# A recurrent mixing layer with a routed expert layer behind it: the output bias added to x in memory by accumulating DMAs, and the row statistics of every block taken by accumulators and ScalarE's squares

## The reference

```
xk, xv, xr = x_prev + (x - x_prev) * tm{k,v,r}        # x_prev: x one token earlier
k, v, r = xk @ Wk + bk, xv @ Wv + bv, xr @ Wr + br
wkv = scan over the tokens of (k, v, time_decay, time_first)
x1 = layernorm(x + (sigmoid(r) * wkv) @ Wo + bo)      # bo: one row of 512 numbers
expert = argmax(softmax(x1 @ wg)); gate = its probability
out = layernorm(x1 + gate * (x1 @ W[expert] + b[expert]))
```

## Time and profile before

| | |
|---|---|
| median of 3 runs | 649.12 us |
| the profiled execution | 652.63 us, its span 650.8 us |
| mean granted TensorE clock of the span | 0.96 |
| TensorE matmul / weight load busy | 582.5 us (90%) / 430.4 us (66%) |
| VectorE busy | 552.7 us (85%) |
| ScalarE busy | 409.4 us (63%) |
| GpSimd busy | 280.3 us (43%) |
| DMA mean rate | 104 GB/s, 67.64 MB |

### The profile page before, as it was taken

The page is one execution under the profiler, slowest core; times in us unless marked ns, Lnnn a source line. Parts: engine busy times, 40 slices in busy tenths (PEclk is TensorE's granted clock), DMA queues, the critical chain, the costliest instruction groups (busy, mean ns, idle before and its releaser), DMA issues. The chain is left out here.

```text
span 650.8 us, 8971 instructions
## 1 busy us (share of the span) xinstructions
PE 582.5 (90%) x2484; PEld 430.4 (66%) x2485; DVE 552.7 (85%) x871; ACT 409.4 (63%) x759; POOL 280.3 (43%) x213
## 2 busy tenths in 40 slices
PE   0667788999999999999999999999998999898991
PEld 0455576667668767677866876875566778676771
DVE  7958898999999899899999989878969698556771
ACT  4246565566756747746775674846957676666883
POOL 5643552552454444445155244421041465555541
PEclk9779898999999999999999999989979999899996
DMA  8030010013104103202210410616834686676660
GB/s 307 18 129 2 1 65 0 1 36 126 34 2 158 37 1 113 64 16 89 72 32 13 150 33 0 227 36 255 259 100 143 185 240 206 204 208 198 201 195 4
DMA packets 36566, 67.64 MB, mean 104 GB/s; under 512 B 8560, under 2 KB 8560, under 8 KB 36532
## 3 DMA queue, kind: packets, MB, share of 16 engines
q1 hardware_dynamic: 30292, 48.29, 23.5%
q0 software_dynamic: 6240, 18.94, 9.1%
HBM read 50.17 MB, written 18.88 MB: 106 GB/s over the span
## 5 line engine op out<-in xcount | busy, mean ns | idle before, releaser
L1110 POOL TENSOR_TENSOR mixed<-unsplit,mixed 128x1024 fp32r<-128x1024 f32 x44 | 104.4, 2392 | 132.4 <-ACT mixed L764 132.4
L512 PE MATMUL kb<-mixed,w_kvr 128*128 128x512 f32 x384 | 99.0, 409 | 23.6 <-DVE mixed L1453 16.6
L512 PE MATMUL vb<-mixed,w_kvr 128*128 128x512 f32 x384 | 102.6, 418 | 14.6 <-DVE evn L1291 9.0
L694 PE MATMUL y_ps<-w_e_hi,xgT 128*128 x312 | 110.4, 414 | 4.2 <-DVE yo L1743 3.2
L512 PE MATMUL rb<-mixed,w_kvr 128*128 128x512 f32 x384 | 102.0, 416 | 5.6 <-DVE ee L1305 4.5
L512 PEld LDWEIGHTS kb<-mixed,w_kvr 128*128 128x128 f32 x384 | 74.4, 197 | 42.2 <-issue 16.2
L530 PE MATMUL y_ps<-w_o,rw 128*128 128x512 f32 x224 | 100.6, 592 | 0.0
L512 PEld LDWEIGHTS vb<-mixed,w_kvr 128*128 128x128 f32 x384 | 74.5, 198 | 36.1 <-DVE evn L1291 11.8
L512 PEld LDWEIGHTS rb<-mixed,w_kvr 128*128 128x128 f32 x384 | 73.5, 194 | 27.9 <-issue 5.7
L1120 POOL TENSOR_TENSOR ee<-ee,state 128x512 f32<-128x512 f32 x32 | 34.9, 1091 | 107.3 <-DVE state L1275 106.6
L1242 DVE SCALAR_TENSOR_TENSOR unsplit<-diff,vec,xb 128x512 f32<-128x512 f32 x96 | 72.1, 812 | 8.1 <-PE kb L512 6.1
(11 more groups left out here) (240 smaller groups left out, 1053.9 us busy)
## 6 DMA issues: line engine op xcount, KB each, us to landing
bias<-b_experts SPq DMA_DIRECT2D x39, 256.0 KB
w_e_raw<-w_experts SPq DMA_DIRECT2D x8, 1024.0 KB, 7.9
rows<-x SPq DMA_DIRECT2D x28, 256.0 KB, 2.6
x_rows<-rows SPq DMA_DIRECT2D x28, 256.0 KB, 2.1
xb<-xT SPq DMA_DIRECT2D x4, 1026.0 KB, 5.4
xb<-xT SPq DMA_DIRECT2D x3, 1024.0 KB, 5.0
w_raw<-w_square SPq DMA_DIRECT2D x2, 1024.0 KB, 10.2
xb<-xT SPq DMA_DIRECT2D x2, 512.0 KB, 5.0
```

The source lines that it names most:

```text
L512: mm = pe.matmul(bank, w_kvr[m][:, a, h, o:o + P], mixed[m][:, bb, h, :], start=(k == 0), stop=(k == 3 * CH - 1))
L694: mm = pe.matmul(y_ps[:, n % 2, :], xgT[n % 3][:, a, c, :], w[:, bass.ds(p, 1), c, :].rearrange("p u o -> p (u o)"), start=(c == 0 and (a, ...
L1110: pool.tensor_tensor(mixed[m][:, LO, 2 * hp:2 * hp + 2, :], unsplit[m][:, LO, 2 * hp:2 * hp + 2, :], mixed[m][:, HI, 2 * hp:2 * hp + 2, :] ...
```

## The change

The bias moves out of the matmuls. A new tensor in device memory, `x_biased`, gets a copy of x, 1 MB for each block, by a DMA of SP (memory to memory); then GpSimd issues an accumulating DMA that adds bo, broadcast over 512 rows, to that copy. `load_rows` and the last block's loads read `x_biased` in place of x. The bias matmuls, `bo2`, and bo's split at the start go away. The way to statistics that the block before the last has is used in all blocks: `add_rows` takes the accumulator, `average` replaces `statistics` and `aggregate`, and ScalarE's `deviation` squares the two row tiles into the tile `x1T`, which serves as scratch, before its Ln and Exp.

```diff
@@ sync @@
+            def copy_block(n, half):
+                sp.dma_start(sum_block[n], x_block[n]).then_inc(x_copied[half], 16)
-                    sp.dma_start(rows[:, j], x_v[n * TPB + j]).then_inc(row_loaded[j], 16)
+                    sp.dma_start(rows[:, j], sum_v[n * TPB + j]).then_inc(row_loaded[j], 16)
             (step)
                 load_x(i + 1, s.batch + s.half, 1 - s.half)
+                if not s.prev2:
+                    copy_block(i + 1, 1 - s.half)
                 if not s.prev:
+                    sp.wait_ge(x_summed[0], 16)
                     load_rows(0, range(TPB), first=True)
                 if s.prev2:
+                    wait_apart(sp, x_summed[1 - s.half], (s.batch + s.half) * 16)
+                    copy_block(i + 1, 1 - s.half)
                     load_rows(m, (0, 1))
             (start)
-            sp.dma_start(b_raw[:], bo).then_inc(bo_loaded, 16)
-            sp.wait_ge(b_lo, 1)
-            sp.wait_ge(bias_zero, 1)
-            for s in range(2):
-                sp.dma_start(bo2[s:s + 1, :].bitcast(F32), b_split[:, s, :].bitcast(F32)).then_inc(bias_moved, 16)
+            copy_block(0, 0)
             (last block)
+            sp.wait_ge(x_summed[0], BATCH * 16)
+            sp.wait_ge(x_summed[1], BATCH * 16)
-                sp.dma_start(rows_last[:, j], x_v[last * TPB + j]).then_inc(last_loaded, 16)
+                sp.dma_start(rows_last[:, j], sum_v[last * TPB + j]).then_inc(last_loaded, 16)
@@ tensor @@
-            def bias_out(bank):
-                pe.matmul(bank, ones[:], bo2[:], start=True, stop=False)
-                bias_out(y_ps[:, j % 2, :])
-                                   start=False, stop=(c == CH - 1))
+                                   start=(c == 0), stop=(c == CH - 1))
             (and the same in out_last, the last block's output projection)
@@ scalar @@
             def deviation(n, h):
                 act.wait_ge(stats_done, n * TPB + (2 * h + 2))
-                act.activation(rstd[:, two], stats[:, two, 1], ACT.Ln, bias=eps_t[:]).then_inc(var_ln, 1)
+                wait(act, logits_done, n * TPB)
+                for j in range(2 * h, 2 * h + 2):
+                    wait_apart(act, squares_done, n * TPB + j)
+                    act.activation(x1T[:].rearrange("p c q -> p (c q)"), rows[:, j], ACT.Square, bias=mean[:, j:j + 1],
+                                   accum_out=rstd[:, j:j + 1]).then_inc(squares_done, 1)
+                wait_apart(act, squares_done, n * TPB + (2 * h + 2))
+                act.activation(rstd[:, two], rstd[:, two], ACT.Ln, bias=eps_t[:], scale=1.0 / H).then_inc(var_ln, 1)
-            act.wait_ge(bo_loaded, 16)
-            act.activation(b_split[:, HI], b_raw[:], ACT.Copy).then_inc(b_hi, 1)
@@ gpsimd @@
+            def add_out_bias(n, batch, half):
+                wait_apart(pool, x_copied[half], batch * 16 + 16)
+                pool.dma_start(sum_block[n], bo[0:1, :].rearrange("u h -> (u h)").partition_broadcast(TB),
+                               accum_op=ALU.add).then_inc(x_summed[half], 16)
                 leave(i, 0)
+                add_out_bias(i, s.batch, s.half)
                 leave(i, 1)
@@ vector @@
             def add_rows(n, j):
-                dve.tensor_tensor(rows[:, j], rows[:, j], y_ps[:, j % 2, :] ..., ALU.add).then_inc(y_taken, 1)
+                dve.scalar_tensor_tensor(out=rows[:, j], in0=rows[:, j], scalar=1.0, in1=y_ps[:, j % 2, :],
+                                         op0=ALU.mult, op1=ALU.add, accum_out=row_sum[:, j:j + 1]).then_inc(y_taken, 1)
+            def average(n, h):
+                dve.wait_ge(y_taken, n * TPB + (2 * h + 4))
+                dve.tensor_scalar(mean[:, two], row_sum[:, two], -1.0 / H, None, ALU.mult).then_inc(stats_done, 2)
             def shift(n, h):
-                dve.scalar_tensor_tensor(out=nmr[:, two], in0=stats[:, two, 0], scalar=-1.0, in1=rstd[:, two],
-                                         op0=ALU.mult, op1=ALU.mult).then_inc(nmr_ready, 1)
+                dve.tensor_tensor(nmr[:, two], mean[:, two], rstd[:, two], ALU.mult).then_inc(nmr_ready, 1)
-            def statistics(n, j):  ... dve.bn_stats(bn[:, j, :], rows[:, j])
-            def aggregate(n, j):   ... dve.bn_aggr(stats[:, j, :], bn[:, j, :])
-            dve.memset(bo2[:].bitcast(F32), 0.0).then_inc(bias_zero, 1)
-            dve.wait_ge(b_hi, 1)
-            dve.tensor_tensor(b_split[:, LO], b_raw[:], b_split[:, HI].bitcast(F32), ALU.subtract).then_inc(b_lo, 1)
-            dve.wait_ge(bias_moved, 32)
```

More of the change, by code:

```diff
@@ L102, in build @@
 def build(nc, x, xT, w_square, w_experts, vectors, bo, b_experts, wg, out):
+    x_biased = nc.dram_tensor("x_biased", [TOKENS, H], F32, kind="Internal").ap()
     x1_rows = nc.dram_tensor("x1_rows", [TOKENS + 1, ROW], F32, kind="Internal").ap()
@@ L155, in build @@
         x1T = place("x1T", [P, CH, P], F32)
-        bo2 = place("bo2", [P, H], F32R)
         ident = place("ident", [P, P], F32)
@@ L165, in build @@
         carry = place("carry", [P, CH, 3], F32)
-        bn = place("bn", [P, TPB, 6], F32)
-        stats = place("stats", [P, TPB, 2], F32)
         rstd = place("rstd", [P, TPB], F32)
@@ L309, in build @@
         x_first, w_k_loaded = [sem(f"x_first{n}") for n in range(2)], [sem(f"w_k_loaded{n}") for n in range(2)]
-        bias_zero = sem("bias_zero")
-        wg_loaded, bias_moved, zero_stored = sem("wg_loaded"), sem("bias_moved"), sem("zero_stored")
+        x_copied, x_summed = [sem(f"x_copied{n}") for n in range(2)], [sem(f"x_summed{n}") for n in range(2)]
+        wg_loaded, zero_stored = sem("wg_loaded"), sem("zero_stored")
         consts_set, decay_exp, vec_ready = sem("consts_set"), sem("decay_exp"), sem("vec_ready")
-        w_hi, w_lo, b_hi, b_lo = sem("w_hi"), sem("w_lo"), sem("b_hi"), sem("b_lo")
-        ident_zero, ident_ready, bo_loaded = sem("ident_zero"), sem("ident_ready"), sem("bo_loaded")
+        w_hi, w_lo = sem("w_hi"), sem("w_lo")
+        ident_zero, ident_ready = sem("ident_zero"), sem("ident_ready")
         x_loaded, x_padded, diffed, mixed_f32 = sem("x_loaded"), sem("x_padded"), sem("diffed"), sem("mixed_f32")
@@ L366, in build @@
         xT_v = xT.rearrange("b (c p) t -> b p c t", p=P)
-        x_v = x.rearrange("b (n p) h -> (b n) p h", p=P)
+        x_block = x.rearrange("b (n q) h -> (b n) q h", q=TB)
+        sum_block = x_biased.rearrange("(n q) h -> n q h", q=TB)
+        sum_v = x_biased.rearrange("(n p) h -> n p h", p=P)
         x1_v = x1_rows[0:TOKENS, 0:H].rearrange("(n p) h -> n p h", p=P)
@@ L637, in out_last @@
                     pe.wait_ge(y_taken, last * TPB + (j - 1))
-                bias_out(bank)
                 for c in range(CH):
-                    mm = pe.matmul(bank, rw[:, HALVES - 1, c, j * P:(j + 1) * P], w_o[:, c, :], start=False, stop=(c == CH - 1))
+                    mm = pe.matmul(bank, rw[:, HALVES - 1, c, j * P:(j + 1) * P], w_o[:, c, :], start=(c == 0), stop=(c == CH - 1))
                 mm.then_inc(y_filled, 1)
@@ L972, in deviation_before @@
                 two = slice(2 * h, 2 * h + 2)
-                act.wait_ge(row_means, h + 1)
+                act.wait_ge(stats_done, before * TPB + (2 * h + 2))
                 squares_of(rows[:, 2 * h], 2 * h)
@@ L985, in deviation_last @@
             def deviation_last(j):
-                act.wait_ge(row_means, j + 3)
+                act.wait_ge(row_means, j + 1)
                 squares_of(rows_last[:, j], TPB + j)
@@ L1182, in _ @@
             mix_lo(last, R, 1)
-            for c in range(CH):
+            leave(last, 0)
+            add_out_bias(last, BATCH - 1, 1)
+            for c in range(1, CH):
                 leave(last, c)
@@ L1329, in result, with add_rows @@
                                          in1=er[:, p], op0=ALU.mult, op1=ALU.mult).then_inc(wkv_done, 1)
-            def add_rows(n, j, bank=None):
+            def add_rows(n, j):
                 dve.wait_ge(row_loaded[j], n * 16 + 16)
                 dve.wait_ge(y_filled, n * TPB + (j + 1))
-                dve.tensor_tensor(rows[:, j], rows[:, j], y_ps[:, j % 2, :] if bank is None else bank, ALU.add).then_inc(y_taken, 1)
+                dve.scalar_tensor_tensor(out=rows[:, j], in0=rows[:, j], scalar=1.0, in1=y_ps[:, j % 2, :],
+                                         op0=ALU.mult, op1=ALU.add, accum_out=row_sum[:, j:j + 1]).then_inc(y_taken, 1)
+            def average(n, h):
+                two = slice(2 * h, 2 * h + 2)
+                dve.wait_ge(y_taken, n * TPB + (2 * h + 4))
+                dve.tensor_scalar(mean[:, two], row_sum[:, two], -1.0 / H, None, ALU.mult).then_inc(stats_done, 2)
             def shift(n, h):
@@ L1354, in add_two @@
                 add_rows(n, 2 * h + 1)
[L1355 to L1358, removed]
+                average(n, h)
             def recurrence(i, c):
@@ L1416, in step @@
                 if s.prev:
[L1417 to L1420, removed]
+                    average(m, 1)
```

(12 more changed lines are left out.)

11 lines of the change are left out of this document (1 added, 10 removed).

## The result

The changed kernel takes 643.81 us in the median (642.44 to 646.49, 8 executions), the kernel before 649.12 (648.45 to 651.63, 8 executions) beside it: ratio 0.9914, 95% interval 0.9893 to 0.9935. So it is faster by 5.3 us, where 11.4 were forecast. The time lies at the upper end of the range, which reaches it only through the two rivals: the forecast's own bounds end at 641.5. On another chip, later, the ratio was 0.9884 (0.9857 to 0.9912). The profiled execution took 642.59 us (span 640.9). That is near the low end of its kind, as the one of before was at the high end of its own, so I don't compare the two spans, but stretches that lie within them.

The account below looks back on a forecast made before the run. Two nearly equal chains, TensorE's own work and one through VectorE, were taken to bound the blocks. Start 0.3, step 1 1.4, blocks 7.8 and end 1.9 sum to 11.4 us, giving a 637.7 us median; range 632 to 645.

Parts of the forecast that it names:

- the two rivals: Blocks: ScalarE's squares decide (643 us, chance 0.16), or TensorE is not the floor (about 633 us, chance 0.10).
- The issue by GpSimd: Accumulating DMA before `leave(i, 1)`: 3.8 us taken, 3.8 to 11.6 possible, 16.5 allowed; hidden, cost nothing.
- the 0.42 us that I gave it: Second pair in a block: `shift` waits 0.42 us, as ScalarE comes 1.70 later and VectorE 1.34 earlier.
- Blocks: From 159.31 to near 410 us: 4.7 periods, each 1.65 us shorter without bias matmuls, saving 7.8 us; bounds 5.1 to 11.7.
- TensorE decides, with 0.7 us to spare: Third k chunk: `distance` gains 0.92 us and ends near 318.7, TensorE by its own work arrives at about 319.4.
- nothing in their way: Twelve matmuls without waits take 2.72 us start to start; the k chunk's 3.23 therefore holds 0.51 us of waiting.
- The rival that lets a third chain, ScalarE's gate among them, hold the period: Blocks stay at 53.4 us a period, only end and start gain 2 us: 647 us, chance 0.09.
- the rival of the squares: Second pair in blocks: ScalarE's squares come 1.7 us later, 1.0 stays uncovered per period: 643 us, chance 0.16.
- priced with its accumulator at 0.20 us a pair: VectorE's statistics, 1.54 us a pair, give way to accumulator and average at 0.20: saves 1.34 a pair, 2.7 a block.
- step 1: VectorE sets its pace and loses 2.7 us; about half, 1.4 us, taken as saved, between 0.9 and 2.7.
- End: Behind the blocks: seven bias matmuls at 0.27 us where VectorE's routing or gathered tiles wait: 1.9 us, between 0.5 and 2.5.
- Start: bo's subtraction on one partition goes, but GpSimd's hold meets the next VectorE instruction: 0.3 us, between 0 and 5.0.

Follow-up runs that it names:

- the statistics alone: Kernel before with only the accumulators, average and ScalarE's squares; bias matmuls stay and rows load from x: ratio 0.9948, period 53.23 us.
- both moves: Changed kernel, chunk 0's gate cap and denominator behind chunk 2's distance, its ScalarE gate exponential behind chunk 1's weights and carry: ratio 0.9798, period 51.88 us.
- the late exponential: ScalarE's exponential of chunk 0's gate behind chunk 1's weights and carry, added to the changed kernel with cap and denominator already moved: ratio 0.9798.
- the gate is late: Changed kernel with chunk 0's gate cap and denominator moved behind the distance of chunk 2 on VectorE: ratio 0.9888, period 52.24 us.
- the bias part alone: Kernel before with copies, accumulating DMAs and no bias matmuls, old statistics: ratio 0.9907, period 52.57; with cap and denominator of chunk 0 moved later, 0.9861, 52.32.
- without the averages: Changed kernel without the average in the blocks, its factors of H folded into the squares, Ln and shift: ratio 0.9873, step 1 51.74 us.
- the kernel before with late gate and exponential: Kernel before with chunk 0's gate cap and denominator behind chunk 2's distance, its exponential behind chunk 1's carry: ratio 0.9901, period 52.83 us.

## Why the forecast was too large

**Right.** The direction. TensorE's own work: forecast at 52.87 less 1.08, measured at 52.80 less 0.96. The issue by GpSimd (3.8 us taken, 1.00 measured), the landing of the accumulates, the row loads: all hidden. The squares didn't hold anything in the blocks: `shift` starts at 305.66, directly behind the `distance` of chunk 1 and without the 0.42 us that I gave it, though ScalarE's Exp had ended only 0.13 us before (305.33 plus 0.20).

**Blocks: 5.5 (4.7 x 1.17) instead of 7.8 us. The step that failed is "TensorE decides, with 0.7 us to spare".** I let `distance` come 0.92 us earlier because VectorE has less to do at the end of a block. But its work up to `distance` begins with `weigh_entry`, which waits for a v chunk that TensorE itself fills just then (wait 0.26 us after, 1.15 with the statistics alone). What VectorE saves ahead of that point turns into waiting there. From it, two ways lead to the third k chunk, one through VectorE's 16.4 us and one from the r chunk through ScalarE's gate and carry; both were level with TensorE's work to 0.1 us, and both start from TensorE, so they shrink only where TensorE is faster. They keep 52.27 - 51.88 = 0.39 us a block, shown by moving two instructions of one and one of the other: the first move by itself gave 0.03, the second was not run by itself. The other 0.09 of the 0.48 a block that the forecast missed is TensorE's own work (51.88 and not 51.79).

Where the 0.39 us lie can be read by comparing a block group by group with the kernel that has both moves. From the v chunk to the third k chunk it is 2.98 against 2.87; behind that k chunk, which waited, the next chunk follows after 2.85 against 2.72; and at chunk 2 the logits and the v chunk behind them take 0.15 more (309.72 to 313.52, 3.80, against 304.78 to 308.43, 3.65). These logits read the turned rows that ScalarE copies behind the same carry. In the changed kernel:

```profile
311.88 0.59 ACT L855 ACTIVATE x1T<-t_ps 128x512 f32<-128x512 f32 x1
```

```profile
312.62 1.05 PE L545 MATMUL lists_ps<-wgs,x1T 128*128 128x8 f32 x8
```

With both moves:

```profile
305.84 0.60 ACT L855 ACTIVATE x1T<-t_ps 128x512 f32<-128x512 f32 x1
```

```profile
307.62 0.95 PE L545 MATMUL lists_ps<-wgs,x1T 128*128 128x8 f32 x8
```

The copy ended 0.15 us ahead of the logits and now ends 1.18 us ahead. So the way through ScalarE seems to reach TensorE at two places, the logits and the third k chunk; the late exponential relieves both, and no run separates them. It also shows that my 2.72 us for "nothing in their way" was too short behind this v chunk, where TensorE with no wait takes 2.87: 0.15 of the 0.51 that I called waiting was its own work, and 0.14 of waiting stood in the chunk behind (2.86 for 2.72), so the two errors nearly cancel in the 52.87.

The change of the statistics is worth 0.2 to 0.3 us a block (0.21 alone, 0.30 on top of the bias part), and 0.1 once the gate is late (52.32 with the bias part alone). The rival that lets a third chain, ScalarE's gate among them, hold the period named one of the two ways; it had the period at 53.4, where most of the gain was kept. That the median falls near the rival of the squares (643) is chance: they decide nothing in the blocks.

**The average, priced with its accumulator at 0.20 us a pair** from a place with no GpSimd instruction beside it, where it reads

```profile
455.29 0.17 DVE L1555 TENSOR_SCALAR mean<-row_sum 128x2 f32<-128x2 f32 x1
```

It measured 0.97 and 1.18 us in the blocks. In them the error cost nothing, since it fills the wait for the v chunk. In step 1 (0.96 and 1.43 us), where VectorE has no such wait, it took 0.5 of the 1.4 us forecast. Another part went to a `shift` that waits for ScalarE's squares (0.19 us after; 1.41 without the averages). Step 1 gave 0.2 to 0.3.

**End: nothing instead of 1.9 us.** The bias matmuls behind the blocks are not where TensorE is last. ScalarE's queue is, here the changed kernel's:

```profile
449.34 1.06 ACT L830 ACTIVATE er<-ee 128x1024 f32<-128x1024 f32 x1 [2.90 <-DVE ee L1314]
...
463.69 0.57 ACT L855 ACTIVATE x1T<-t_ps 128x512 f32<-128x512 f32 x1
```

```profile
464.40 1.03 PE L545 MATMUL eb<-wgs,x1T 128*128 128x8 f32 x8 [1.06 <-ACT x1T L855]
```

From the last reciprocal's guess ScalarE works 14.35 us without a gap to the turned rows, with two of the experts' conversions in between; in the kernel before, it was 14.28 (454.38 to 468.66). TensorE, without its bias matmuls, waits 1.06 us for it where it had no wait before. That the matmuls give nothing there is shown by this wait in every kernel without them; I ran no kernel that changes ScalarE's queue there. From that guess to VectorE's copy of TensorE's list it is 24.16 us before (454.38 to 478.54), and 23.99 and 24.55 in the changed kernel's two profiles.

**Start: 0.3 forecast, nothing shown.** Profiles of one kernel differ by more.

The sum by rows: step 1 0.2, the four periods 4.7, the rest up to 410 us 1.0 (36.59 to 35.62 from the third k chunk of block 6 to chunk 1 of block 7), and from there to ScalarE's guess -0.3: 5.6 us, against 5.3 measured. It leaves out what stands ahead of step 1, where the changed kernel's profile is 0.6 us later (107.42 against 106.84): the start's 0.7, less 0.1 in step 0.

## What to carry to other kernels

Before you credit a cut to the chain that sets the pace, find where that chain starts: what lies ahead of a wait for the engine that you take to be the floor turns into more of that wait. Two engines that arrive together need both ways shortened, and the queue order of a third may hold a way that no wait of the first two shows; follow the last arrival back through all of them. And a duration is only good for the neighbours it had: look at what GpSimd does at the new place of a VectorE instruction.

## What the hardware showed that I had not expected

A VectorE instruction of two elements a partition was held for up to 1.43 us, to the end of GpSimd's instruction of 2.4 us, in two of three forms; with an accumulator to write it took 0.14 to 0.16 us beside the same instruction. The old pair of aggregates was not held either: in the kernel before with late gate and exponential it took 0.42 us from 298.53, 0.55 us into a low half that ran from 297.98 to 300.40. A copy in memory of 1 MB and an accumulate of 1 MB in each block raised the DMA engines' share from 0.18 to 0.39 and the row loads from 2.6 to 3.9 us; the stores of finished rows went from 2.1 to 7.0 us (2.7 and 2.1 us again without the traffic). Period and step 1 were the same without all of it.
